# A two-stage convolution block on one core: one right-neighbour and one diagonal product of group 0 recast by F(2,2), one product per group formed from banded DMA sums and ScalarE squares

## The reference, cut to what matters

```python
def _gn(v, G=32, eps=1e-05): ...          # normalises each of the 32 channels of an image by itself
def _L0_conv_ref(x, w3, b3, w5, b5, wr, br):
    y3 = conv3x3(x, w3) + b3;  y5 = conv5x5(x, w5) + b5
    # nine shifts of y3 and y5, weighted per channel by wr, plus br
def _L1_conv_ref(x, filters):              # filters: (32, 32, 10, 10)
    # spot = [1, the nine pixels of the 3x3 window]; feat = outer product of spot with itself
    out = einsum('bcyxf,ocf->boyx', feat, filters)
x = x + _L0_conv_ref(_gn(x), ...)          # x: (8, 32, 64, 64)
x = x + _L1_conv_ref(_gn(x), filters)
```

## Time and profile before

| | before |
|---|---|
| median of 3 runs | 294.31 us (293.18 to 294.38) |
| profiled execution | 294.57 us, span 292.8 us |
| PE busy | 271.2 us, 93% of the span |
| DVE busy | 254.4 us, 87% |
| ACT, POOL busy | 94.6 us, 31.1 us |
| granted TensorE clock, mean | 0.992 |
| chain that ended last | PE 68%, DVE 15%, ACT 8% |

### The profile page before, as it was taken

One profiled execution on the slowest core, in us unless ns is written; L12 is line 12 of the kernel. 1 busy time (PEld: TensorE's weight loads), 2 busy tenths in 40 slices (PEclk: granted clock), 3 DMA queues, 4 the chain that ended last, 5 costly groups with the idle time before them and its releaser, 6 DMA issues.

```text
span 292.8 us, 13506 instructions
## 1 busy us (share of the span) xinstructions
PE 271.2 (93%) x6416; PEld 127.8 (44%) x6416; DVE 254.4 (87%) x224; ACT 94.6 (32%) x137; POOL 31.1 (11%) x87
## 2 busy tenths in 40 slices
PE   0499999999998999999999999999999999999990
PEld 0233443444434434454447477344343454654740
DVE  3999799999999969798999999999999999974203
ACT  4532005999159789819600000000450000000000
POOL 5704990000110000000000000000000000000000
PEclk9999999999999999999999999999999999999996
DMA  6975000000000000000000000039100000000067
GB/s 173 380 212 115 3 4 2 2 6 2 2 2 4 4 2 2 2 4 2 3 4 2 4 2 4 2 77 193 26 2 2 4 2 4 2 4 2 17 133 143
DMA packets 19462, 11.45 MB, mean 39 GB/s; under 512 B 18000, under 2 KB 18128, under 8 KB 19280
## 3 DMA queue, kind: packets, MB, share of 16 engines
q1 hardware_dynamic: 14768, 9.06, 12.3%
q10 hardware_dynamic: 4640, 1.53, 2.2%
HBM read 6.40 MB, written 4.19 MB: 36 GB/s over the span
## 4 chain that ended last, share of the span: by engine, by line
PE 68%; DVE 15%; ACT 8%; issue 5%; DMA 1%; SPq 0%; DVEq 0%
PE acc L1127 62%; ACT raw L557 6%; PE acc L1170 5%; DVE stats L816 3%; DVE plane L834 2%; DVE scaled L710 1%; DVE product L710 1%; ACT edges L575 1%; DVE raw L894 1%; DMA w_in<-in_L_conv_w 1%; PE acc L1221 1%; DVE product L977 1%; DVE product L742 1%; DVE product L736 1%; DVE arena L742 1%
## 5 line engine op out<-in xcount | busy, mean ns | idle before, releaser
L1127 PE MATMUL acc<-product,weight 32*32 32x512 f32 (+1 forms) x3040 | 127.6, 604 | 0.3 <-DVE product L977 0.3
L1127 PEld LDWEIGHTS acc<-product,weight 32*32 32x32 f32 (+1 forms) x3040 | 65.3, 110 | 58.1 <-issue 41.2
L989 DVE TENSOR_TENSOR product<-plane 128x4096 f32<-128x4096 f32 x15 | 65.9, 4428 | 0.1
L1170 PE MATMUL acc<-product,middle 32*64 32x512 f32 (+1 forms) x576 | 30.1, 597 | 0.2 <-ACT edges L575 0.2
L1127 PE MATMUL acc<-raw,weight 32*32 32x512 f32 (+1 forms) x608 | 29.4, 603 | 0.0
L594 ACT ACTIVATE scaled<-acc 128x2048 f32<-128x2048 f32 x2 | 3.8, 1880 | 61.9 <-PE acc L1127 61.9
L557 ACT ACTIVATE raw<-arena 32x512 f32<-32x512 f32 x32 | 21.8, 681 | 0.5
L1127 PE MATMUL acc<-product,arena 32*32 32x512 f32 (+1 forms) x448 | 21.2, 604 | 0.0
L710 DVE TENSOR_TENSOR product<-plane 128x2048 f32<-128x2048 f32 (+1 forms) x8 | 20.0, 2507 | 0.0
L557 ACT ACTIVATE raw<-product 32x512 f32<-32x512 f32 x28 | 18.9, 675 | 2.7 <-DVE product L742 2.3
L816 DVE BATCH_NORM_STATS2 stats<-raw 128x6 f32<-128x512 f32 x32 | 19.6, 677 | 0.1
(11 more groups left out here) (142 smaller groups left out, 279.9 us busy)
## 6 DMA issues: line engine op xcount, KB each, us to landing
raw<-in_x SPq DMA_DIRECT2D x8, 512.0 KB, 8.5
out<-raw SPq DMA_DIRECT2D x16, 128.0 KB, 2.9
arena<-in_L_conv_filters SPq DMA_DIRECT2D x4, 400.0 KB, 7.1
out<-raw SPq DMA_DIRECT2D x16, 64.0 KB, 2.4
out<-raw ACTq DMA_DIRECT2D x16, 64.0 KB, 2.8
arena<-in_L_conv_w ACTq DMA_DIRECT2D x4, 100.0 KB, 3.8
w_in<-in_L_conv_w ACTq DMA_DIRECT2D x2, 36.0 KB, 1.8
w_in<-in_L_conv_w SPq DMA_DIRECT2D x2, 36.0 KB, 2.3
```

The source lines that it names most:

```text
L989: nc.vector.tensor_tensor(both_halves(g, u), plane_halves(g), plane_halves(g, PRODUCTS[k][0] * PITCH + PRODUCTS[k][1]), ALU.mult)\
L1127: return nc.tensor.matmul(acc[32 * s:32 * (s + strips), j, r, :], weights[32 * r:32 * r + 32, t:t + strips, :] .rearrange("p t c -> p (t c ...
L1170: return nc.tensor.matmul(acc[32 * s:32 * (s + strips), odd, r, :], five[32 * r:32 * r + 32, t:t + strips, :].rearrange("p t c -> p (t c)" ...
```

## The change

Group 0 gets group 1's treatment of `NEXT` and `DIAGONAL`: one shared call (`whole_products`, new, for both groups) with summed taps in j = 0 alone, and left and right half streams for each j (`side_units`). That adds four half streams on DVE in group 0, a new order of units on DVE and PE, new homes, and `keep_cross(0)` ahead of `keep_sum(0)` on ACT. Unit 13 (`ADDED`) is no longer multiplied: with a the plane and b the shifted plane, ab = ((a+b)^2 - a^2 - b^2)/2, so SP copies `plane[g]` in six bands to `added_planes`, POOL issues six accumulating transfers onto them, each waited for, and ACT squares the result (`square_added`); POOL halves unit 13's taps and subtracts them from those of the square. The x of group 0 comes in 8 pieces instead of 4, the warm-up has 2 + 1 rounds instead of 3 + 1 and waits for piece 5 of 8, the identity matrix is summed on POOL instead of DVE, and the two tiles of `w3` lie in `added_planes`. `mix(0)` moves behind unit 17. `evict(0, 0)` stands ahead of `multiply(1, NEXT)` and `evict(0, 1)` right behind it.

```diff
-    PIECES = 4
+    PIECES = (8, 4)
+        added_planes = sb("added_planes", [128, PLANE_LEN])
+        w3_in = added_planes[:, 0:C * 9]
...
             sp.wait_ge(piece_in[1][PIECES[1] - 1], 16)
...
+            for g in range(NG):
+                sp.wait_ge(plane_dve, NG + g + 1)
+                sp.wait_ge(plane_act, NG + g + 1)
+                if g == 1:
+                    sp.wait_ge(added_squared, 1)
+                for n in range(PARTS):
+                    sp.dma_start(band(added_planes, n), band(plane[g], n)).then_inc(plane_copied, 16)
+                    sp.wait_ge(plane_copied, 16 * (PARTS * g + n + 1))
...
+            pool.wait_ge(eye_ready, 2)
+            nc.gpsimd.tensor_tensor(eye_from[:, 0:2, :], eye_wide[:, 0:2, :], eye_wide[:, 2:4, :], ALU.add)\
+                .then_inc(eye_ready, 1)
...
+            added_taps = sums[:, FIRST1[ADDED - 5]:FIRST1[ADDED - 5] + 2, :]
+            nc.gpsimd.tensor_scalar(added_taps, added_taps, 0.5, None, ALU.mult).then_inc(halved, 1)
+            pool.wait_ge(halved, 4)
+            for a in (FIRST1[0], FIRST1[0] + 7):
+                last = nc.gpsimd.tensor_tensor(sums[:, a:a + 2, :], sums[:, a:a + 2, :], added_taps, ALU.subtract)
...
+            def add_planes(g, parts):
+                d = PRODUCTS[ADDED - 5]
+                for n in parts:
+                    pool.wait_ge(plane_copied, 16 * (PARTS * g + n + 1))
+                    pool.dma_start(band(added_planes, n), band(plane[g], n, d[0] * PITCH + d[1]), accum_op=ALU.add)\
+                        .then_inc(planes_added, 16)
+                    pool.wait_ge(planes_added, 16 * (PARTS * g + n + 1))
+
+            add_planes(0, range(PARTS))
             pool.wait_ge(plane_dve, NG + 2)
             pool.wait_ge(plane_act, NG + 2)
             stream_borders(raw[1]).then_inc(borders, 1)
+            add_planes(1, range(PARTS - 3))
             pool.wait_ge(stream_made, made(0, LAST_UNIT))
             stream_borders(home(1, NEXT)).then_inc(borders, 1)
+            add_planes(1, range(PARTS - 3, PARTS))
...
+            def square_added(g):
+                act.wait_ge(planes_added, 16 * PARTS * (g + 1))
+                act.wait_ge(borders, (4, 6)[g])
+                wait_used(act, g, (8, DIAGONAL_SIDES)[g])
+                nc.scalar.activation(view(home(g, ADDED), 0, (HPITCH, H + 2), (HALF_LEN, 2), (1, HPITCH)),
+                                     view(added_planes, PITCH, (PITCH, H + 2), (1, 2), (2, HPITCH)), ACT.Square)\
+                    .then_inc(added_squared, 1)
...
-            pe.wait_ge(piece_in[0][2], 16)
-            warm_up(3)
+            pe.wait_ge(piece_in[0][5], 16)
+            warm_up(2)
...
+            def whole_products(g, forms):
+                diagonal_rows = rows_of(PRODUCTS[DIAGONAL - 5])
+                for pairs in forms:
+                    wait_made(g, NEXT)
+                    column(0, stream_pixels(g, NEXT, 0), every_row, next_sum, False, False, pairs)
+                    wait_made(g, DIAGONAL)
+                    last = column(0, stream_pixels(g, DIAGONAL, 0), diagonal_rows, diagonal_sum, False,
+                                  pairs == forms[1], pairs)
+                last.then_inc(shared_done, 1)
```

More of the change, by code:

```diff
@@ L92 @@
-USED = ([LINEAR, SQUARE_MIXED, LINEAR_SIDES, SQUARE_SIDES, NEXT] + list(range(7, LAST_UNIT)),
-        [LINEAR, SQUARE_MIXED, LINEAR_SIDES, SQUARE_SIDES, NEXT_SIDES, DIAGONAL_SIDES] + list(range(8, LAST_UNIT)))
-MADE = (["square sum", "linear cross", "square cross", "linear left", "next", "square left", "linear right",
-         "square right", 7, 8] + list(range(10, LAST_UNIT + 1)),
-        ["linear sum", "linear cross", "square sum", "square cross", "next", "linear left", "linear right", DIAGONAL,
-         "square left", "square right", "next left", "next right", "diagonal left", "diagonal right", 8]
-        + list(range(10, LAST_UNIT + 1)))
+ADDED = 13
@@ new lines @@
+USED = [LINEAR, SQUARE_MIXED, LINEAR_SIDES, SQUARE_SIDES, NEXT_SIDES, DIAGONAL_SIDES] + list(range(8, LAST_UNIT))
+SIDES_MADE = ["square left", "square right", "next left", "next right", "diagonal left", "diagonal right", 8]\
+    + [u for u in range(10, LAST_UNIT + 1) if u != ADDED]
+MADE = (["square sum", "linear cross", "square cross", "next", DIAGONAL, "linear left", "linear right"] + SIDES_MADE,
+        ["linear sum", "linear cross", "square sum", "square cross", "next", "linear left", "linear right", DIAGONAL]
+        + SIDES_MADE)
@@ L277, in plane_half, with band @@
             return view(plane[g], PLANE_AT + col, (PITCH, H), (2, HALF_W))
+        def band(tile, n, shift=0):
+            at = PITCH + n * BAND + shift
+            return tile[:, at:at + BAND]
         def half_at(g, name):
@@ L1111, in _ @@
             mix(1)
-            for u in range(10, LAST_UNIT + 1):
+            for u in (10, 11, 12, 14, 15, 16, 17):
                 multiply(1, u)
@@ L1305, in side_unit, with side_units @@
                               start, False, pairs)
+            def whole_products(g, forms):
[7 more added lines that the diff above has]
+                last.then_inc(shared_done, 1)
+            def side_units(g, forms):
+                one, other = forms
+                pe.wait_ge(shared_kept, 2 * g + 1)
+                side_unit(g, 1, "linear", one, start=True)
+                side_unit(g, 1, "linear", other)
+                pe.wait_ge(shared_kept, 2 * g + 2)
+                side_unit(g, 0, "linear", other, start=True)
+                side_unit(g, 0, "linear", one).then_inc(unit_used, 1)
+                side_unit(g, 0, "square", one)
+                side_unit(g, 1, "square", one)
+                side_unit(g, 0, "square", other)
+                side_unit(g, 1, "square", other).then_inc(unit_used, 1)
+                side_unit(g, 0, "next", other)
+                side_unit(g, 1, "next", other)
+                side_unit(g, 0, "next", one)
+                side_unit(g, 1, "next", one).then_inc(unit_used, 1)
+                side_unit(g, 0, "diagonal", one)
+                side_unit(g, 1, "diagonal", one)
+                side_unit(g, 0, "diagonal", other)
+                side_unit(g, 1, "diagonal", other).then_inc(unit_used, 1)
             def taps1(g, j, u, pairs, stop=False):
@@ L1355, in _ @@
                     mixed_unit(g, 0, "square", SINGLES)
-                    mixed_unit(g, 0, "square", PAIRS, stop=True).then_inc(shared_done, 1)
+                    mixed_unit(g, 0, "square", PAIRS)
                     pe.wait_ge(edges_copied, 2 * NG)
```

145 lines of the change are left out of this document (61 added, 84 removed).

## The result

The changed kernel took 289.8 us in the median of 4 runs (288.5 to 290.18), the kernel before on the same chip 294.35 (293.18 to 294.57): ratio 0.9846, 95% interval 0.9805 to 0.9887. Run again on two other chips it took 290.79 against 293.9 (0.9891, 0.9869 to 0.9913) and 290.17 against 294.3 (0.9871, 0.9845 to 0.9896). So the change is worth 3.1 to 4.5 us by these medians. The forecast of 289.4 us is met within 0.4 us beside the kernel before that it was made for; the forecast gain of 4.9 us was not reached on any chip. The profiled execution is the fastest of its four, 288.5 us with a span of 286.6.

A forecast was written before the change was run, and what follows sets the result against it. PE was taken to bound stage 1 from 108.60 us while DVE keeps ahead. Terms -4.9 - 0.3 + 0.3 + 0.1 + 0.3 - 0.4 = -4.9 gave 289.7 from 294.57, forecast 289.4 us for the median; range 288.1 to 292.6.

The forecast's parts named there:

- What bounds the kernel: From 108.60 to 277.3 us one unbroken piece of PE matmuls, so saved PE calls save time while DVE keeps ahead.
- PE calls saved: Group 0 of stage 1: right neighbour 2.89 us less and diagonal 2.02 less on PE, together -4.9 us.
- the gap: PE's 0.28 us wait for the square side stream goes, as calls needing only finished units come first: -0.3 us.
- Unit 12: Group 0: DVE ends it at 151.4 and PE wants it at 151.3, a dead heat; stall of +0.3 us.
- Group 1's diagonal: DVE has it at 201.1 and PE wants it at 201.0, a tie costing 0 to 0.2, taken as +0.1 us.
- The transfers' sums: Unit 13's copies and accumulating transfers: 5 us a band, done at 120, up to 10.3 us a band free; cost nothing.
- POOL beside DVE: Three more small POOL operations at 43.6 us beside DVE's critical scale chain and normalisation: +0.3 us, bounds 0 and 1.7.
- The start: DVE's statistics begin earlier, with the identity sum on POOL and x in 8 pieces: -0.4 us.
- DVE binds sooner: Rival, chance 0.15: margins at unit 12, evict(0,1) and group 1's diagonal fail, adding 1 to 2 us: 291.0.
- The clock rises later: Rival, chance 0.10: after the shorter warm-up the first products run at the lower clock level, costing 1.2 us: 290.6.
- The sums hold up PE: Rival, chance 0.07: beyond 10.3 us a band each further microsecond costs 6; at 12 us a band 299.6.
- POOL's issuing blocks DVE: Rival, chance 0.10: writing the transfers' descriptors stops DVE, 1.7 us each giving 299.6, 0.4 each 291.8.

The follow-up runs named there:

- f22_only: Changed kernel with unit 13 multiplied on DVE again, without copies, sums, square or tap subtractions: 293.68 us, ratio 0.9993 to the kernel before.
- before_split: Kernel before with two waits added that split POOL's sums of the first layer's filters: 293.97 us, ratio 0.9989.
- after: The changed kernel as first measured and profiled: 289.8 us in the median, the profiled execution 288.5 us with a span of 286.6.
- parts22: Changed kernel with unit 13's copies and sums in 22 bands of 3 rows instead of 6 of 11: 309.49 us, ratio 1.0519 to the kernel before.
- after_again: The changed kernel run again without edit on a second chip: 290.79 us, against 293.9 for the kernel before.
- pool_late: Changed kernel with POOL's filter sums waiting until DVE has normalised group 1 of stage 0: 290.34 us, ratio 0.9877 to the kernel before.
- pool_split_again: Changed kernel with two waits splitting POOL's filter sums, second measurement, on the third chip: 290.34 us, ratio 0.9888 to the kernel before.

## Why the prediction was right, point by point

*What bounds the kernel*: right, and closer to its end than the one word "PE" says. `f22_only` shows that 4.4 us of DVE work in each group turn the whole gain into waits and a slower clock.

*PE calls saved, -4.9, and the gap, -0.3*: group 0 of stage 1 lost 5.4 us. Of these 0.73 are a stall for instructions at the edge parts, which the kernel before had in its profile and the kernel after did not; `before_split`, without that stall, takes 103.47 us for the group, 4.6 more than `after`. The 4.7 left answer to -4.9 - 0.3 + 0.3 at unit 12, of which 0.1 was paid, and to the 0.25 us at the cross streams, which stood in no term.

*Unit 12, +0.3*: PE wants it at the moment when it is made, as worked out (151.3 against 151.4). Weight loads wait 0.97 us there against 0.84 to 0.89 at the other changes of that form: 0.1 us. *Group 1's diagonal, +0.1*: 0.36 us, the size was low; where PE had lost time before (second chip), it vanished. Group 1 is 0.4 us longer in two profiles and unchanged in the third.

*The transfers' sums, nothing*: right for the waits that it names, not for the whole cost. A band took 4.59 us against 5; done at 115 instead of 120. The threshold of 10.3 us a band is confirmed by `parts22`, where PE wanted unit 13 at 155.9, the square took 4.3 and the sums began at 87.9: 10.6 us a band. What stands behind the sums in POOL's queue is confirmed too. The step asked who waits for a band and not who shares the DMA engines with it: PE's instructions do, and the stalls that go with them are 0.25 us in `after` and 1.1 more in `after_again`. That the bands cause them fits, but is not shown. The Trainium skill (DMA: Bandwidth & Descriptors, Anatomy of one DMA) would have a band's accumulating transfer at 2.9 us, an estimate; the trace has 4.3 from issue to landing, and the measurement decides.

*POOL beside DVE, +0.3*: the three operations themselves cost nothing that shows (stage 1 begins at 88.32 to 88.35 where DVE loses the collision, 88.34 before). What the step missed is that the 1.7 us row itself comes and goes between runs of the same kernel.

*The start, -0.4*: 0 to 0.3 us, half of it lost again in the scale's chain. Together with the step before, -0.1 was predicted up to stage 1, and 0.0 measured in the two profiles without luck.

*Rivals*: "DVE binds sooner" is half true, 0.5 us of waits instead of 1 to 2 (0.1 at unit 12, 0.36 at the diagonal). "The clock rises later" did not come. "The sums hold up PE" has its place and about its price confirmed by `parts22` (8 us of wait by the 70 us for the sums, 6.8 measured), with the bands of the changed kernel far from its threshold. "POOL's issuing blocks DVE" is refuted: 30.51 against 30.52 us; the rule of the Trainium skill (SBUF — State Buffer, Who interferes with whom) holds here.

So the sum's -4.9 stands against -4.7 for the profiled execution on the third chip (289.83 to 294.57) and -6.1 for the first, 1.26 of which is the collision. That the median meets the forecast is partly luck, a cancelling of small errors: POOL's +0.3 and the start's -0.4 were both nearer to nothing, the diagonal cost 0.3 more and the cross streams 0.25, and the 0.73 us stall of the kernel before, which flatters the change, stood in no term. Where the stall in unit 13 came on top, on the second chip, the medians differ by 3.1 us and not by 4.9.

## What to carry to other kernels

Where the chain shows one engine, ask how far behind the next one is: here a saving of 4.9 us on PE was worth 0.2 alone, and it became real only with DVE's work moved to ACT and to DMA engines that had little to do. Little is not nothing: ask what else uses the engine that takes the work, here PE's own instructions. Give a slow helper a limit per piece (10.3 us here) and list what is queued behind it; both were what decided when it was stretched. And before a fraction of a per cent is explained, profile the same kernel twice: its profiles differed by 1.9 us of span, from a collision of DVE with POOL and from late instructions.

## What the runs showed of the hardware

- PE's instructions arrive in 16 KB transfers on a queue of their own over the same DMA engines as the data (49 in `after`, 50 in the kernel before, which has more matmuls). One that began 66 to 68 weight loads late stopped PE's weight loads for 0.9 us (`after_again`, `pool_late`, `pool_split_again`). Short matmuls (32 x 64 and 32 x 1 columns at the edges) waited 0.73 us for instructions in the kernel before with the DMA engines nearly idle (share 0.06 and less from 90 to 93 us).
- A copy and an accumulating transfer of 363, 198 and 99 KB, one after the other with POOL confirming each, repeat every 4.59, 4.15 and 3.23 us: most of it does not shrink with the size.
- When a DVE operation with two SBUF operands meets POOL's sums, which of them is slowed varies between executions of the same kernel: 4.01 and 6.06 us (`after_again`), or 2.29 and 10.16 (`after`); DVE lost in eight of ten profiles. DVE's operations with one operand in PSUM beside the same sums took 2.29 (the kernel before, at 32.18 and 34.50 us).
- After a PE wait of 2.3 us the granted clock was 0.50 for some 3 us (`f22_only`, a loss of 1.4 us); after stalls of 0.9 us it stayed at 1.00 (`after_again`).
